# A fused diffusion, convolution, selective-scan and DCT kernel: the second pair's preparation placed inside the scan, small norm steps on ScalarE

## What is computed

```python
x = x + L0(_gn(x))   # 5 steps of nonlinear diffusion: depthwise 3x3, Sobel, 1/(1+2Bx+2By); BN, relu
x = x + L1(_gn(x))   # dense 3x3 convolution, 64 -> 64, + bias
x = x + L2(_gn(x))   # layer norm, Mamba block, + skip, layer norm, 64x64 projection
x = x + L3(_gn(x))   # 2-D DCT over height and width
```

```python
xi, z = split(x @ in_proj_w.T)
xs = silu(causal_conv4(xi) + conv_b)
dt, B, C = split(xs @ x_proj_w.T)
delta = softplus(dt @ dt_proj_w.T + dt_proj_b)
h_t = exp(delta_t * A) * h_{t-1} + (delta_t * u_t) * B_t     # for each of 16 states
y_t = sum over states of h_t * C_t, + D * u_t
out = (y * silu(z)) @ out_proj_w.T
```

## Time and profile before

| what | us |
|---|---|
| median of 3 runs (lowest, highest) | 1094.13 (1092.56, 1095.31) |
| profiled execution, its own time | 1093.66 |
| its span | 1091.5 |
| busy: PE / DVE / ACT / POOL | 825.2 / 908.3 / 416.7 / 661.0 |
| the last image's preparation up to the first scan step, first half | 39.8 |
| the first scan, first step to last | 247.9 |
| between the two scans, up to the diffusion loop | 102.0 |
| the second scan | 239.1 |
| after the second scan | 55.2 |

### The profile page before, as it was taken

How to read it: one execution, slowest core, us unless ns; L and a number is a source line. 1 busy time by engine, 2 the same in 40 slices (tenths; PEclk the granted TensorE clock), 3 DMA queues, 4 the chain that set the end, 5 groups by cost and what they waited for, 6 DMA issues and landing times.

```text
span 1091.5 us, 6945 instructions
## 1 busy us (share of the span) xinstructions
PE 825.2 (76%) x2210; PEld 379.7 (35%) x2210; DVE 908.3 (83%) x729; ACT 416.7 (38%) x433; POOL 661.0 (61%) x294
## 2 busy tenths in 40 slices
PE   3968998875477776868997799887637786777854
PEld 2423443432133322324444344343212242333433
DVE  5999884489999999999987888447998999999921
ACT  3734331157434232324554433115743433333401
POOL 2446992112788697878452699211268989886910
PEclk9997999998688899899998999898868899998966
DMA  3000000003454455445100000000314555455501
GB/s 95 1 0 0 0 0 1 0 5 106 119 174 158 150 202 182 156 154 193 20 0 13 7 0 0 1 0 5 106 62 171 191 168 210 165 176 163 162 0 19
DMA packets 37807, 91.04 MB, mean 83 GB/s; under 512 B 16264, under 2 KB 16400, under 8 KB 37776
## 3 DMA queue, kind: packets, MB, share of 16 engines
q1 hardware_dynamic: 37456, 89.62, 25.0%
q0 software_dynamic: 320, 1.05, 0.4%
HBM read 87.51 MB, written 3.15 MB: 83 GB/s over the span
## 4 chain that ended last, share of the span: by engine, by line
DVE 45%; PE 33%; issue 9%; POOL 8%; ACT 4%; DMA 0%; DVEq 0%; POOLq 0%; SPq 0%; ACTq 0%
DVE arena L1331 13%; PE ps L649 9%; PE ps L445 7%; DVE ps L1325 7%; PE ps L544 5%; POOL arena L318 5%; ACT arena L753 3%; PE ps L643 3%; DVE arena L1288 3%; PE ps L451 2%; DVE arena L1190 2%; DVE arena L1160 1%; POOL arena L311 1%; PE ps L434 1%; PE ps L590 1%
## 5 line engine op out<-in xcount | busy, mean ns | idle before, releaser
L318 POOL TENSOR_TENSOR arena<-arena 128x1024 f32<-128x1024 f32 x128 | 303.7, 2382 | 84.7 <-DVE arena L1331 69.2
L544 PE MATMUL ps<-arena,mat 128*128 128x512 f32 x512 | 275.0, 665 | 66.0 <-POOL arena L318 53.3
L1331 DVE TENSOR_TENSOR_SCAN arena<-arena,ps 128x1024 f32<-128x1024 f32 x96 | 219.5, 2287 | 12.7 <-POOL arena L318 9.5
L753 ACT ACTIVATE arena<-arena,Amat 128x1024 f32<-128x1024 f32 x96 | 110.2, 1149 | 210.4 <-DVE arena L1331 197.0
L544 PEld LDWEIGHTS ps<-arena,mat 128*128 128x128 f32 x512 | 102.3, 206 | 179.4 <-POOL arena L318 90.2
L753 ACT ACTIVATE arena<-arena 128x1024 f32<-128x1024 f32 (+3 forms) x120 | 76.5, 677 | 157.2 <-DVE arena L1256 74.8
L534 PE MATMUL ps<-arena,sel 96*128 96x512 bf16 x192 | 61.9, 408 | 77.9 <-DVE arena L1331 77.9
L1325 DVE TENSOR_TENSOR ps<-arena,ps 128x1024 f32<-128x1024 f32 x96 | 116.2, 1210 | 2.5 <-POOL arena L311 2.1
L649 PE MATMUL ps<-arena,mat 128*128 128x512 f32 x240 | 106.3, 592 | 0.0
L445 PE MATMUL ps<-arena,diag 128*128 128x512 f32 x192 | 85.9, 606 | 2.1 <-ACT arena L753 2.1
L326 POOL TENSOR_TENSOR arena<-arena,BB 128x1024 f32<-128x1024 f32 x32 | 75.2, 2350 | 0.0
(11 more groups left out here) (149 smaller groups left out, 1353.1 us busy)
## 6 DMA issues: line engine op xcount, KB each, us to landing
arena<-bc_rows SPq DMA_DIRECT2D x128, 512.0 KB, 3.9
...
```

The source lines that it names most:

```text
L318: tt(HC[s % 2], HS[s % 2], CB[s % 4], ALU.mult).then_inc(S("hc"), 1)
L544: last = mm(half(PS[3], n), ident, half(HC[s % 2], n), start=first, stop=True, skip_group_check=True)
L753: return nc.scalar.activation(out_, in_, func, bias=bias, scale=scale)
L1331: nc.vector.tensor_tensor_scan(HS[q], a, b, 0.0, ALU.mult, ALU.add).then_inc(S("scan"), 1)
```

## The change

- Ahead of the scan only pair 0 is prepared, and of pair 1 the first image's x and z and its `causal`. The rest of image 2 and all of image 3's chain go into the scan by step number on each engine: image 2 from step 3 (`silu_x`) to 15, image 3 from step 12 (`in_proj_x`) to 28. `in_proj` and `x_proj` are split into x, z, dt and B/C calls with PSUM tiles of their own (`z_ps`, `bc_ps`). On ACT `layer_scale` of pair 1 now stands ahead of `middle` of image 0; on PE `x_dt` and `x_bc` of image 1 stand ahead of `in_proj` of image 2.
- The third copy of `parts` (B's high part) of pair 1 goes to ACT (`hi_rows`).
- The statistics of x for the next half and of x3 (the last group norm) are made on ACT, as two passes with a sum output (`keep_x_sums`, `x3_sums`), and the small steps behind them too (`small_group_var`, `small_group_shift`). Pair 1's x is transposed at the end of the scan and not in it. In the last layer norm ACT does the scaling of mean and variance (`small_mean`, `small_variance`).
- The centred values of the layer norms stay in PSUM, where `square` and `normalize` read them; the tile XC is gone.
- Between the scans ACT does `reciprocal` of pair 1 and `relu` ahead of `copy_a2` and `copy_out`.
- SP: image 2's and 3's rows are stored at steps 14 and 28, the next x loaded at step 6, pair 0's output stored at step 62.

The core of the diff (12 blanks of indentation taken off; blank lines left out):

```diff
...
+def z_ps(k, b):
+    return [PS[1], PS[1], PS[3], PS[2]][2 * k + b]
+def bc_ps(k):
+    return PS[1 + k]
...
             input_times_b(h, s + 4)
-        if s == 5:
-            relu_part(h, 3)
-        if s in (10, 25):
-            delta_u(h, 2 + s // 16)
-        if h + 1 < HALVES and s in (13, 21):
-            root(A[s // 16], h + 1, 0, s // 16)
-        if s == 38:
+        if s == 3:
+            delta_u(h, 1)
+        if s in (11, 24):
+            relu_part(h, 2 + s // 16)
+        if s in (28, 33):
+            delta_u(h, 2 + s // 32)
+        if h + 1 < HALVES and s == 33:
+            root(A[0], h + 1, 0, 0)
+        if s == 39:
             layer_root(D[0], 4 * h + 3)
-        if s == 50:
+        if s == 51:
             root(D[0], h, 3, 0)
 layer_root(D[1], 4 * HALVES)
...
+    x_dt(h, 0, 0)
+    x_bc(h, 0, 0)
+    in_proj_x(h, 0, 1)
+    in_proj_z(h, 0, 1)
     xn_channels(h, 1)
-    in_proj(h, 1, 0)
-    x_proj(h, 0, 1)
-    x_proj(h, 1, 0)
-    in_proj(h, 1, 1)
+    x_dt(h, 0, 1)
+    x_bc(h, 0, 1)
+    in_proj_x(h, 1, 0)
+    in_proj_z(h, 1, 0)
     pe.wait_ge(S("r10"), 2 * h + 2)
...
         if s == 2 * D_STATE - 2:
-            pe.wait_ge(S("bcs1"), ONE + 2 * h + 2)
+            pe.wait_ge(S("bcs1"), ONE + 4 * h + 4)
             plain(pe)
         b_rows(h, s + 2)
         sum_of(h, s - 1)
-        if h + 1 < HALVES:
-            if s == 5:
-                pe.wait_ge(S("rx1"), 2 * h + 2)
+        if s == 3:
+            x_dt(h, 1, 0)
+        if s == 7:
+            x_bc(h, 1, 0)
+        if s == 12:
+            in_proj_x(h, 1, 1)
+        if s == 15:
+            in_proj_z(h, 1, 1)
+        if s == 18:
+            x_dt(h, 1, 1)
+        if s == 21:
+            x_bc(h, 1, 1)
+        if s == 27:
...
+            pe.wait_ge(S("bcf"), 4 * h + 4)
+            if h + 1 < HALVES:
                 x_channels(h + 1, 0, PS[2])
-            if s == 10:
-                group_mean(A[0], h + 1, 0, 0)
-            if s == 13:
-                pe.wait_ge(S("a_x"), 2 * h + 3)
+        if s == 31 and h + 1 < HALVES:
+            group_mean(A[0], h + 1, 0, 0)
+        if s == 33:
+            if h + 1 < HALVES:
                 pe.wait_ge(S("group0"), g_var(h + 1, 0))
-                x_channels(h + 1, 1, PS[2])
-            if s == 18:
-                group_mean(A[1], h + 1, 0, 1)
...
             keep_x3(h, 0)
             second_dct(h, 0)
-        if s == 62:
+        if s == 61:
             pe.wait_ge(S("ot"), 2 * h + 1)
             skip(1)
+        if s == 62:
             out_proj(h, 2)
+    if h + 1 < HALVES:
+        pe.wait_ge(S("scan"), SCANS * (h + 1))
+        x_channels(h + 1, 1, PS[0])
     sum_of(h, SCANS - 1)
+    if h + 1 < HALVES:
...
+def hi_rows(h, b):
+    cols = slice(b * L, b * L + L)
+    act.wait_ge(S("bcs1"), ONE + 4 * h + 2 * b + 1)
+    av(D[1]["BCS"][0:32, cols], D[1]["HI"][0:32, :], ACT.Identity).then_inc(S("bcs1"), 1)
...
+def small_mean(h, k):
+    m = D[k]["m"]
+    act.wait_ge(S(f"lstep{k}"), 4 * h + 3)
+    av(m[:, :], m[:, :], ACT.Identity, 1.0 / C).then_inc(S("lmean"), 1)
+def small_variance(h, k):
+    v = D[k]["v"]
+    act.wait_ge(S(f"lstep{k}"), 4 * h + 4)
+    av(v[:, :], v[:, :], ACT.Identity, 1.0 / C, par[:, 12:13]).then_inc(S("lvar"), 1)
+def keep_x_sums(h, k):
+    ag = A[k]["ag"]
+    ps = [PS[2], PS[0]][k]
+    act.wait_ge(S("a_xT"), 2 * h + k + 1)
+    av(xres[k][:, :], ps[:, :], ACT.Square, accum_out=ag[:, 1:2]).then_inc(S(f"gstep{k}"), 1)
+    act.wait_ge(S(f"gstep{k}"), 5 * g_count(h, 0) - 4)
+    av(xres[k][:, :], ps[:, :], ACT.Identity, accum_out=ag[:, 0:1]).then_inc(S("a_x"), 1)
+    act.wait_ge(S("a_x"), 2 * h + k + 1)
+    act.sem_inc(S(f"group{k}"), 1)
+def x3_sums(h, k):
+    ag = D[k]["ag"]
+    act.wait_ge(S("X3"), 2 * h + k + 1)
+    av(F[k]["A2"], F[k]["X3"], ACT.Square, accum_out=ag[:, 1:2]).then_inc(S(f"gstep{k}"), 1)
+    act.wait_ge(S(f"gstep{k}"), 5 * g_count(h, 3) - 4)
+    av(F[k]["A2"], F[k]["X3"], ACT.Identity, accum_out=ag[:, 0:1]).then_inc(S(f"group{k}"), 1)
+def small_group_var(t, h, g, k):
+    ag, step, n0 = t["ag"], S(f"gstep{k}"), 5 * g_count(h, g) - 4
+    act.wait_ge(S(f"gmean{k}"), g_count(h, g))
+    av(ag[:, 2:3], g_ps(h, g, k)[:, 0:1], ACT.Identity, -1.0 / L).then_inc(step, 1)
+    av(ag[:, 3:4], g_ps(h, g, k)[:, 1:2], ACT.Identity, 1.0 / L, par[:, 11:12]).then_inc(step, 1)
+    act.wait_ge(step, n0 + 2)
+    av(ag[:, 4:5], ag[:, 2:3], ACT.Square).then_inc(step, 2)
+    act.wait_ge(step, n0 + 4)
+    av(t["gn"][:, 0:1], ag[:, 4:5], ACT.Identity, -1.0, ag[:, 3:4]).then_inc(S(f"group{k}"), 1)
+def small_group_shift(t, h, g, k):
+    act.wait_ge(S(f"grstd{k}"), g_count(h, g))
+    if g == 3:
+        av(t["gn"][:, 1:2], t["ag"][:, 2:3], ACT.Identity, par[:, 13:14]).then_inc(S("root_h"), 1)
+        act.wait_ge(S("root_h"), 2 * h + k + 1)
+        av(t["gn"][:, 1:2], t["gn"][:, 1:2], ACT.Identity, t["gn"][:, 0:1]).then_inc(S(f"group{k}"), 1)
+    else:
+        av(t["gn"][:, 1:2], t["ag"][:, 2:3], ACT.Identity, t["gn"][:, 0:1]).then_inc(S(f"group{k}"), 1)
 def zero_framed(h, k):
...
         act.wait_ge(S("scan"), SCANS * h)
+        keep_x_sums(h, 1)
         first_taps(h, 0)
+        small_group_var(A[1], h, 0, 1)
+        small_group_shift(A[1], h, 0, 1)
+        zero_framed(h, 1)
         squares(h, 0)
+        small_mean(h - 1, 1)
         square(h - 1, 1, 1)
+        small_variance(h - 1, 1)
         reciprocal(h, 0)
         last_scale(h - 1, 1)
         relu(h, 0, 0)
         frames(h, 1)
         first_taps(h, 1)
         from_D(h, 0)
+        x3_sums(h - 1, 1)
+        small_group_var(D[1], h - 1, 3, 1)
         relu(h, 0, 1)
+        small_group_shift(D[1], h - 1, 3, 1)
         copy_x3(h - 1, 1)
         squares(h, 1)
         scale(h - 1, 1)
+        reciprocal(h, 1)
         copy_a2(h - 1, 1)
+        relu(h, 1, 0)
         copy_out(h - 1, 1)
-        reciprocal(h, 1)
-        relu(h, 1, 0)
     from_D(h, 1)
     relu(h, 1, 1)
     for k in range(2):
...
     abs_x(h, 0, 0)
     first_part(h, 0, 0)
     keep_rows(h, 0, 0)
+    layer_scale(h, 1)
     middle(h, 0, 0)
-    layer_scale(h, 1)
     silu_z(h, 0, 1)
     silu_x(h, 0, 1)
     silu_z(h, 1, 0)
     abs_x(h, 0, 1)
-    silu_x(h, 1, 0)
     first_part(h, 0, 1)
+    exp_of(h, 0)
+    exp_of(h, 1)
     keep_rows(h, 0, 1)
-    abs_x(h, 1, 0)
     middle(h, 0, 1)
-    first_part(h, 1, 0)
-    keep_rows(h, 1, 0)
-    middle(h, 1, 0)
-    for j in range(3):
-        exp_of(h, j)
-    silu_z(h, 1, 1)
-    silu_x(h, 1, 1)
-    for j in range(3):
-        ln_of(h, j)
-    abs_x(h, 1, 1)
-    decay(h, 0)
-    first_part(h, 1, 1)
-    keep_rows(h, 1, 1)
-    decay(h, 1)
-    middle(h, 1, 1)
-    decay(h, 2)
-    exp_of(h, 3)
-    decay(h, 3)
-    for s in range(4, SCANS):
+    ln_of(h, 0)
+    ln_of(h, 1)
+    for s in range(SCANS):
         decay(h, s)
-        if s == D_STATE - 1:
+        if s == 3:
+            silu_x(h, 1, 0)
+        if s == 6:
+            abs_x(h, 1, 0)
+            exp_of(h, 2)
+        if s == 10:
+            first_part(h, 1, 0)
+            keep_rows(h, 1, 0)
...
+        if s == 17:
+            silu_z(h, 1, 1)
+            silu_x(h, 1, 1)
+        if s == 20:
+            abs_x(h, 1, 1)
+            exp_of(h, 3)
+        if s == 24:
+            first_part(h, 1, 1)
+            keep_rows(h, 1, 1)
+        if s == 26:
+            middle(h, 1, 1)
+            ln_of(h, 2)
             ln_of(h, 3)
-        if h + 1 < HALVES and s in (8, 16):
-            keep_x(h + 1, s // 16, PS[2])
-        if s == 38:
+        if s == 28:
+            hi_rows(h, 1)
+        if h + 1 < HALVES:
+            if s == 30:
+                keep_x_sums(h + 1, 0)
+            if s == 33:
+                small_group_var(A[0], h + 1, 0, 0)
+            if s == 36:
+                small_group_shift(A[0], h + 1, 0, 0)
+        if s == 39:
+            small_mean(h, 0)
             square(h, 0, 1)
-        if s == 44:
+        if s == 41:
+            small_variance(h, 0)
+        if s == 45:
             last_scale(h, 0)
-        if s == 53:
+        if s == 49:
+            x3_sums(h, 0)
+        if s == 51:
+            small_group_var(D[0], h, 3, 0)
+        if s == 54:
+            small_group_shift(D[0], h, 3, 0)
             copy_x3(h, 0)
         if s == 56:
             scale(h, 0)
-        if s == 59:
+        if s == 58:
             copy_a2(h, 0)
-        if s == 62:
+        if s == 61:
             copy_out(h, 0)
     if h + 1 < HALVES:
         act.wait_ge(S("X3"), 2 * h + 1)
         zero_framed(h + 1, 0)
         frames(h + 1, 0)
-        zero_framed(h + 1, 1)
 h = HALVES - 1
...
 square(h, 1, 1)
+small_variance(h, 1)
 last_scale(h, 1)
+x3_sums(h, 1)
+small_group_var(D[1], h, 3, 1)
 copy_x3(h, 1)
+small_group_shift(D[1], h, 3, 1)
...
-    d, step, n0 = D[k], S(f"lstep{k}"), 6 * h + 3 * g
-    xc, ps = [D, F][g][k]["XC"], PS[2] if g == 1 else PS[2 * k]
+    d, step, n0 = D[k], S(f"lstep{k}"), 4 * h + 2 * g
+    ps = PS[2] if g == 1 else PS[2 * k]
```

(80 more changed lines are left out.)

152 lines of the change are left out of this document (76 added, 76 removed).

## The result

| | before | after |
|---|---|---|
| median (lowest, highest), 4 runs each | 1093.64 (1092.56, 1095.31) | 1116.21 (1113.19, 1119.95) |
| profiled execution, its span | 1091.5 | 1114.1 |

The ratio is 1.0207, 95% interval 1.0173 to 1.0241. The forecast was 1104, with a range up to 1115: slower was right, but the loss is 22.6 us and not 10.5. The interval leaves open whether it is more or less than 2%.

The account below looks back on a forecast made before the run. VectorE's own work was taken to bound the scans, single waits the stretch between them. Before the scans +5.4, inside +1.1, between +4, ends 0: +10.5 on 1093.66 gives 1104.2, forecast 1104 us, range 1088 to 1115.

Parts of the forecast that it names:

- Ahead of the scan: Before each scan: later chain, VectorE idle some 13 us, first step at 278.7; +2.7 us a half, +5.4 in all.
- both reasons: Before the scan: layer_scale ahead of middle delays parts 3.8 us; PE's and ScalarE's orders put image 1's dt behind image 2's z.
- The locks: In the scan: VectorE instructions reading two SBUF tensors wait for GpSimd; one_plus 4.9 us, parts 2.1, delta 2.2.
- never seen waiting: Argument for the faster rival: one_plus's 0.67 us tensor_scalar, seen only in a quiet stretch, doesn't wait for GpSimd.
- the locks don't bite: Faster rival: moved instructions keep quiet prices in the scans, 10.1 us less a half, 1084 us; chance 0.19.
- Idle in the scans: VectorE's idle in each scan: 6.5 us, from 3.4 at step 6 and as much again over the rest.
- one 3.4 us wait at step 6: In the scan: VectorE idles 3.4 us because GpSimd does delta_u of image 1 behind step 3 with input_times_b.
- Between the scans: Center idles 4.7 us for ScalarE, copy_a2 at about 593, last merge 4 to 5 us late: +4, bounds -3 to +7.
- VectorE's gain on the way to the denominator: Between the scans: statistics, a wait and the locked shift go (-6.6 us), second sobel's work some 3 us earlier.
- side effect of one swap: Between the scans: reciprocal ahead of copy_a2 puts copy_a2 behind the denominator, from 588.16 to about 593; merge 4 to 5 late.
- The decays come late: Slower rival in the scans: ScalarE's decays 2 to 3 us late at three places a half, +15, 1119 us; chance 0.19.
- 21.0 and 9.3 us leave, 16.7 come in twice: VectorE's busy time in the scans: moved work adds 16.7 us each; net -4.3 in the first, +7.4 in the second.

Follow-up runs that it names:

- e1: Changed kernel with ScalarE's middle of image 0 back in front of layer_scale of pair 1 ahead of the scan: 1104.56 us.
- e2: Changed kernel with PE's x and z projections of image 2 in front of dt and B/C of image 1 ahead of the scan: 1107.66 us.
- e3: Changed kernel with ScalarE's small_mean of the last image's norm ahead of the squares of image 0 between the scans: 1114.59 us.
- e4: Changed kernel with ScalarE's copy_a2 of pair 1 in front of reciprocal of pair 1 between the scans: 1112.66 us.
- e8: Changed kernel with ScalarE's small_mean ahead of the squares, and copy_a2 and copy_out ahead of reciprocal of pair 1, between the scans: 1102.52 us.
- e5: Changed kernel with GpSimd's delta_u of image 1 at step 8 of the scan instead of step 3: 1109.11 us.

## Why the prediction fell short

- **Ahead of the scan: right.** Idle of 13.52 us ended by ScalarE, first step at 279.11 against 278.7, and both reasons hold (e1, e2). In the second half the stage grew by 0.5 where 2.7 stood. That is no steady difference: VectorE's wait was 1.6 us shorter there because TensorE's second projection happened to be fast, and the same code took 178.4 to 179.2 us in e3, e4 and e8, which is +3.2 to +3.9.
- **The locks: right.** one_plus took 2.12 + 3.25 us in the first scan and 0.67 + 3.26 the second time, 4.9 were taken. By the rule of the Trainium skill, "SBUF — State Buffer", section "Who interferes with whom", its tensor_scalar waits too; the trace agrees, 2.12 us against 0.69 in a quiet stretch. The one of 0.67 began while GpSimd stood idle. The prediction counted it for the rival that a tensor_scalar was "never seen waiting", but the L1155 of the earlier trace rows is one, with 1.32 us for 16 columns. The rival "the locks don't bite" is out.
- **Idle in the scans: the term that was mis-sized.** 6.5 us taken for each, 13.2 and 13.5 measured. I counted one 3.4 us wait at step 6 and put as much again for everything else, without a row for it. The wait was there, 3.1 us (e5), but beside it came waits for the rows of B, the root, the gate and the projection: 6.5 us in the first scan. They are smaller in the first scans of e1, e2 and e5, which also have a higher granted clock on TensorE, but the changed kernel's second scan has the higher clock of its two (0.89) and not less idle, so the clock as their cause isn't shown. With 3.4 us of busy time taken too high this makes 10.2 of the missing 12 us. e5 accounts for 5.4 us of the extra idle in the first scan and for 1.6 in the second; the rest of it stays without a proven cause.
- **Between the scans: right chain, too short.** center's 5.0 us (4.7 forecast) were on the path (e3), and the merge waited for copy_a2 through TensorE, as I had it. But I had copy_a2 at 593 and the merge 4 to 5 us late. Counted from the last scan step copy_a2 came 5 us later than that and the merge 10.2 us later than before; 1.9 of these were gained back behind the merge: +8.3 for +4. The step that failed is VectorE's gain on the way to the denominator, which I had 3 us earlier and which came 1.6 us later than before. VectorE was ahead until 581.45; there it waited 2.25 us for GpSimd, and its two instructions for the x neighbours took 3.22 and 3.24 us beside GpSimd's instructions where they had taken 1.21 each. The locks that I had priced inside the scan weren't in this sum. What I named as a side effect of one swap was the largest single thing on the path here: e8, which undoes this order, gives 15.3 us of that stretch back.
- **"The decays come late": not seen.** It gave 1119, close to what was measured, for a reason that isn't there: VectorE waited 0.4 us at most for a decay in a scan.
- **The balance.** The prediction never gave a time for either part of the change by itself. Its own rows had them: 21.0 and 9.3 us leave, 16.7 come in twice.
